# Transposes and value products in pairs, with a score block between, in a fused attention and feed-forward kernel

## The chip, the cores and the metric

The kernel runs on one NeuronCore of a Trainium2 chip. The metric is the device time of one execution in microseconds (us), lower is better. TensorE is PE in the profile, VectorE is DVE, ScalarE is ACT, GpSimd is POOL and SyncE is SP.

## What is computed

One transformer layer on x of 2 batches x 1024 positions x 256 channels, in float32, with adaptive layer norm (the six modulations come from a small input c):

```python
h = _layernorm(x) * (1 + ca) + sa
qkv = einsum('bsh,ph->bsp', h, weight_qkv)         # 4 groups: 4 query heads, 1 key, 1 value, D = 128
scores = einsum('bsgqd,btgd->bgqst', q, k) * D ** -0.5
attn = softmax(where(causal, scores, min))
out = einsum('bgqst,btgd->bsgqd', attn, v)
x = x + ga * (out @ weight_proj.T)
h = _layernorm(x) * (1 + cb) + sb
x = x + gb * ffn(h)                                # two Hadamard transforms, gate and up, silu, down
```

## The kernel before

**Precision.** Every float32 product is made of three matmuls on numbers split in a high and a low part: high x high, high x low, low x high (helper `three`, lines 1127 to 1129, and their like). So everything that TensorE multiplies is first split by two instructions: ACT copies the high part, and DVE subtracts it to get the low one. Transposes are plain float32.

**Turns.** Attention runs in 8 turns (2 batches x 4 key-value groups). One turn holds the queries, keys and values of one group in SBUF. Its 8 rows of 128 positions are taken in four windows, (7,0), (6,1), (5,2), (4,3). A unit (i, j) is row i against key block j for all four heads; there are 36 in a turn, numbered in `UNITS`, 9 in a window. After the turns the feed-forward part runs; the change leaves it alone.

**The walk.** The order of the work is one list, `WALK`, made by `walk()` (line 74). Each engine's program goes through the same list and issues its own share of each item, in order. Items of a turn, written below as in the code with their index:

- C c: chunk c of the next turn's queries, keys (6 matmuls each) or values (12). ACT and DVE split it.
- S i.h: scores of row i, head h (lines 1267 to 1273; 3 or 6 matmuls, row 0 in plain float32 at L1263). DVE takes the maximum (L1040), ACT the exponential (L778), POOL the reciprocal of the sum (L623) and the scaling (L628). There are two score buffers in PSUM, so a score block waits on `exp_done` for the exponential of the block two before it (line 1257; in rows under 4, heads 2 and 3 use the other half and wait for the one four before).
- T n: four transposes of unit n into one of two PSUM banks (L1284). ACT copies it to `pt_hi` (L802), DVE makes `pt_lo` (L1044). The bank is free when `pt_lo` of the unit two before is made; the layer-norm transposes L take a place in the same ring.
- V n: value product of unit n, three matmuls of 512 columns (L1302, L1303, L1305). The first two wait for `pt_hi`, the third for `pt_lo`. After the last unit of a row ACT and DVE split the sum (L819, L1049).
- Y i: output projection of row i, 12 matmuls of 256 columns; DVE adds it to x (L1054). The first of a turn, Y 0, waits on `wp_ready` for the projection weights (line 1311).
- WM and WP: POOL scales the projection weights (L606), and splits them (L614, L616). WP comes before the turn's Y 0.
- VS: ACT and DVE split the values. LF, LN, L, LH, LL: layer norm of two blocks for the feed-forward part: statistics and normalising on DVE, transposes on PE (L), modulation on ACT in the item L (L706), the copy h_hi on DVE in the item LH (L905), the low part on POOL. The bank of L is free when L706 is done. W: POOL splits the next turn's query and key weights (before every second turn the value weights too).

**Exponentials.** ACT doesn't issue the exponential of a score block in that block's item. It keeps it in the list `waiting`, which `exps()` empties: at the next S, C, VS or L item, and after the copy of a T.

**Order before.** A value product follows its transposes at a distance of two units (`LAG = 2`). In the middle of a turn one has S, T n, V n-2, S, T n+1, V n-1, and so on. In the last window the next turn's chunks take the place of the score blocks. In the first turn the items WM and WP stand ahead of the scores of row 7.

Of the kernel before, what the change touches and what calls it, by code (L numbers as in the profile page):

```python
# [70 lines left out]
CHUNKS_AT = [(4, 4, 3, 3), (3, 3, 2, 2)]  # L71


def walk():

# [10 lines left out]
    out += [(0, "C", 9, 0), (0, "WM", 0, 0), (0, "WP", 0, 0), (0, "C", 10, 0)] + s7[:2]  # L91
    out += [(0, "C", 11, 0)] + s7[2:] + [(0, "C", 12, 0), (0, "C", 13, 0)]
    for t in range(TURNS):
        s0, s6 = scores(t, 0), scores(t, NT - 2)
# [3 lines left out]
        behind, due = [], []

        def value():  # L100
            n = behind.pop(0)
            out.append((t, "V", n, 0))
            if due and due[0][0] == 1:
                out.append((t, "Y", due.pop(0)[1], 0))
            for row in due:
                row[0] -= 1
            if n == LAST[UNITS[n][0]]:
                due.append([3 if n >= NU - 3 else 2, UNITS[n][0]])

        for p, pair in enumerate(WINDOWS):  # L110
            units = [n for n, u in enumerate(UNITS) if u[0] in pair]
            fill = [[] for _ in units]
            if p + 1 < NW:
                for k, item in enumerate([item for i in WINDOWS[p + 1] for item in scores(t, i)][p == 0 and t > 0:]):
                    fill[k + (p == 0) * (1 if not t else (k > 1) + (k > 2))].append(item)
            elif t + 1 < TURNS:
                left = [(t + 1, "C", c, 0) for c in range(len(chunks(t + 1)))]
                for k, many in enumerate(CHUNKS_AT[(t + 1) % 2]):
                    fill[k] += left[:many]
                    del left[:many]  # L120
                for h, item in enumerate(scores(t + 1, NT - 1) + scores(t + 1, 0)[:1]):
                    fill[len(CHUNKS_AT[0]) + h].append(item)
                fill[1].append((t + 1, "WM", 0, 0))
            if p == 1:
                for k, what in ((0, "LF"), (3, "LN"), (5, "L"), (6, "LH"), (7, "LL")):
                    fill[k].append((t, what, 0, 0))
# [1291 lines left out]
```

## Time and profile before

| | |
|---|---|
| median of 3 runs | 930.82 us (930.01 to 933.1) |
| the profiled execution's own time | 929.75 us |
| its span, first to last instruction | 927.9 us |
| mean granted TensorE clock | 0.998 of full |
| busy: PE, DVE, ACT, POOL | 98%, 68%, 56%, 53% |
| attention turns | about 47 us to 780 us of the span |

A row of the timeline gives the start in us from the span's start, the time that it took, the engine, the source line, the operation, what it writes and reads, the shape and how many alike are merged. In square brackets stands the idle time of the engine just before it and what ended it. The end of a matmul is modelled and includes its way through the array, so a matmul "takes" 0.27 us and the next one starts 0.11 us after it: the spacing of starts is what a matmul costs TensorE, and a wait shorter than that way through is not listed as idle.

### The profile page before, as it was taken

What the parts mean: (1) busy time and instruction counts of PE and PEld (TensorE: products, weight loads), DVE (VectorE), ACT (ScalarE), POOL (GpSimd) and SP (SyncE); (2) the same over time, 40 slices, a digit from 0 to 9 for tenths busy, and PEclk for the clock granted to TensorE, in tenths of its full rate; (3) what the DMA queues carried; (4) which work ended last, traced back from release to release, by engine and by line L of the source; (5) the groups of instructions that cost most, each with busy time, mean ns of one, the idle gap of its engine ahead of it and who ended that gap; (6) DMA issues with size and microseconds to landing.
All of it is one profiled execution on the core that took longest, in us unless ns stands there. A gap on an engine that the chain in (4) does not pass through costs nothing.

```text
span 927.9 us, 15010 instructions
## 1 busy us (share of the span) xinstructions
PE 911.6 (98%) x5480; PEld 806.3 (87%) x5480; DVE 629.5 (68%) x1297; ACT 515.5 (56%) x1121; POOL 490.0 (53%) x699
## 2 busy tenths in 40 slices
PE   6989999999999999999999999999999999999997
PEld 5888889888898888888888888888888998888886
DVE  6568667865787578647875787378757776764554
ACT  4366556655766576547664766466647667531111
POOL 1576628671867186808671867166727989410000
PEclk9999999999999999999999999999999999999999
DMA  8000100000001000000010000000001001000000
GB/s 283 24 1 2 40 1 24 1 29 1 23 2 40 1 23 1 29 1 23 2 41 1 24 1 29 1 1 24 1 1 69 1 9 67 1 23 0 23 23 23
DMA packets 10180, 21.21 MB, mean 23 GB/s; under 512 B 1280, under 2 KB 5760, under 8 KB 9984
## 3 DMA queue, kind: packets, MB, share of 16 engines
q1 hardware_dynamic: 9392, 20.11, 6.3%
q8 instruction: 41, 0.67, 0.3%
q10 hardware_dynamic: 720, 0.21, 0.1%
q14 instruction: 27, 0.22, 0.1%
HBM read 18.22 MB, written 2.10 MB: 22 GB/s over the span
## 4 chain that ended last, share of the span: by engine, by line
PE 88%; DVE 3%; ACT 2%; POOL 1%; issue 1%; DVEq 0%; POOLq 0%
PE ps L1284 13%; PE ps L1127 12%; PE ps L1129 12%; PE ps L1128 12%; PE ps L1305 6%; PE ps L1302 6%; PE ps L1303 6%; PE ps L1267 6%; PE ps L1273 6%; PE ps L1270 6%; ACT prob L778 1%; DVE ps L1040 1%; ACT pt_hi L802 1%; DVE stats L881 1%; PE ps L1263 1%
## 5 line engine op out<-in xcount | busy, mean ns | idle before, releaser
L623 POOL TENSOR_TENSOR rinv<-rsum,mone 128x1 f32<-128x1 f32 x256 | 141.4, 552 | 232.0 <-ACT prob L778 231.4
L1044 DVE TENSOR_TENSOR pt_lo<-ps,pt_hi 128x512 fp32r<-128x512 f32 x288 | 198.2, 689 | 66.6 <-ACT pt_hi L802 63.4
L802 ACT ACTIVATE pt_hi<-ps 128x512 fp32r<-128x512 f32 x288 | 171.3, 598 | 118.2 <-PE ps L1284 115.8
L778 ACT ACTIVATE prob<-ps,nmax 128x256 f32<-128x256 f32 (+28 forms) x256 | 180.8, 706 | 84.2 <-DVE nmax L1040 82.4
L628 POOL TENSOR_SCALAR prob<-prob,rinv 128x256 f32<-128x256 f32 (+28 forms) x256 | 191.3, 747 | 38.8 <-POOL rinv L623 38.5
L1040 DVE CUSTOM_DVE_ANT_0 ps<-ps,mask_f 128x256 f32<-128x256 f32 (+28 forms) x256 | 183.1, 719 | 37.7 <-PE ps L1273 33.9
L1284 PE MATMUL ps<-ident,prob 128*128 128x128 f32 x1152 | 173.0, 274 | 2.7 <-POOL prob L628 2.4
L1284 PEld LDWEIGHTS ps<-ident,prob 128*128 128x128 f32 x1152 | 140.9, 141 | 22.8 <-DVE pt_lo L1044 4.0
L1302 PE MATMUL ps<-pt_hi,v_hi 128*128 128x512 f32 x288 | 134.3, 466 | 0.0
L1305 PE MATMUL ps<-pt_lo,v_hi 128*128 128x512 f32 x288 | 114.1, 396 | 0.0
L1303 PE MATMUL ps<-pt_hi,v_lo 128*128 128x512 f32 x288 | 113.4, 394 | 0.0
L1267 PE MATMUL ps<-k_hi,q_hi 128*128 128x256 f32 (+16 forms) x352 | 101.1, 346 | 0.6
L1273 PE MATMUL ps<-k_hi,q_lo 128*128 128x256 f32 (+16 forms) x352 | 98.0, 337 | 0.0
L1270 PE MATMUL ps<-k_lo,q_hi 128*128 128x256 f32 (+16 forms) x352 | 97.6, 337 | 0.0
L982 DVE SCALAR_TENSOR_TENSOR q_lo<-ps,q_hi 128x512 fp32r<-128x512 f32 x64 | 44.2, 692 | 53.2 <-ACT q_hi L739 53.1
L1267 PEld LDWEIGHTS ps<-k_hi,q_hi 128*128 128x128 f32 x352 | 63.0, 190 | 15.8 <-ACT prob L778 5.5
L1127 PE MATMUL ps<-wp_hi,o_hi 128*128 128x256 f32 x256 | 73.1, 285 | 0.0
L1129 PE MATMUL ps<-wp_hi,o_lo 128*128 128x256 f32 x256 | 72.4, 283 | 0.0
L1128 PE MATMUL ps<-wp_lo,o_hi 128*128 128x256 f32 x256 | 72.2, 282 | 0.0
L829 ACT ACTIVATE prob<-ps,ws_u 128x512 f32<-128x512 f32 x32 | 22.0, 688 | 87.7 <-PE ps L1129 87.6
L1270 PEld LDWEIGHTS ps<-k_lo,q_hi 128*128 128x128 f32 x352 | 64.1, 189 | 5.3
L1049 DVE TENSOR_TENSOR o_lo<-ps,o_hi 128x512 fp32r<-128x512 f32 x64 | 44.2, 691 | 34.3 <-ACT o_hi L819 34.3
(179 smaller groups left out, 1815.8 us busy)
## 6 DMA issues: line engine op xcount, KB each, us to landing
w_raw<-in_wqkv SPq DMA_DIRECT2D x8, 640.0 KB, 3.9
wp_raw<-in_wproj SPq DMA_DIRECT2D x8, 512.0 KB, 3.5
out_y<-prob SPq DMA_DIRECT2D x8, 256.0 KB, 2.3
x<-in_x SPq DMA_DIRECT2D x3, 512.0 KB, 12.9
prob<-in_wug SPq DMA_DIRECT2D x3, 512.0 KB, 4.0
prob<-in_wmod SPq DMA_DIRECT2D x1, 1024.0 KB, 10.2
wv_raw<-in_wv SPq DMA_DIRECT2D x4, 256.0 KB, 4.3
raw_down<-in_wdn SPq DMA_DIRECT2D x1, 1024.0 KB, 4.8
```

The source lines that it names most:

```text
L628: g_.tensor_scalar(row(i, h), row(i, h), rinv[:, at, h:h + 1], 1.0, ALU.mult, ALU.mult).then_inc(prob_done, 1)
L778: a_.activation(row(i, h).rearrange("p (a n) -> p a n", a=nb), score_banks(i, h).rearrange("p (a n) -> p a n", a=nb)[:, :, 0:w], ACT.Exp, ...
L802: a_.activation(pt_hi[:, n % 3, :], ring(t, "T", n), ACT.Copy).then_inc(pth_done, 1)
L1040: v_.tensor_tensor_reduce(scores, scores, late, -1.0, 3.0e38, ALU.add, ALU.min, nmax[:, place(n), h:h + 1]).then_inc(max_done, 1)
L1044: v_.tensor_tensor(pt_lo[:, n % 3, :], ring(t, "T", n), pt_hi[:, n % 3, :].bitcast(F32), ALU.subtract).then_inc(ptl_done, 1)
L1127: mm(dst, w_h, r_h, start=start, stop=False)
L1128: mm(dst, w_h, r_l, start=False, stop=False)
L1129: return mm(dst, w_l, r_h, start=False, stop=stop)
L1267: mm(dst[:, a * CH:a * CH + wide], queries(q_hi, n, h), k_hi[:, a * w:a * w + wide], start=True, stop=False)
L1270: mm(dst[:, a * CH:a * CH + wide], queries(q_hi, n, h), k_lo[:, a * w:a * w + wide], start=False, stop=False)
L1284: last = tr(ring(t, "T", n)[:, q * P:(q + 1) * P], row(i, q, j * P, (j + 1) * P), ident[:, :])
L1302: mm(O[i], v_hi[:, j, :], pt_hi[:, n % 3, :], start=j == 0, stop=False)
```

## The change

The walk is written anew. Units are taken in pairs g = (2g, 2g+1): what is to stand ahead, T 2g, T 2g+1, what is to stand between, V 2g, V 2g+1, what is to stand behind. The function `put` gives each score block, chunk and layer-norm item a place; an even place n is ahead of pair n/2, an odd one is between the transposes and the value products of pair (n-1)/2. Counted out, turns 1 to 6 read (with | around the pairs' T and V for the eye):

```text
S7.3 V34 V35 Y3 S0.0 S0.1 S0.2 S0.3 VS Y4 WP S6.0 | T0 T1 | S6.1 | V0 V1 | T2 T3 | S6.2 | V2 V3 | T4 T5 | S6.3 Y0 | V4 V5 |
S1.0 | T6 T7 | S1.1 | V6 V7 | S1.2 | T8 T9 | S1.3 S5.0 LF | V8 V9 | S5.1 | T10 T11 | S5.2 Y7 | V10 V11 | LN | T12 T13 | S5.3 | V12 V13 |
S2.0 | T14 T15 | S2.1 LH Y1 | V14 V15 | L S2.2 | T16 T17 | S2.3 LL | V16 V17 | S4.0 | T18 T19 | S4.1 Y6 | V18 V19 | T20 T21 | S4.2 W | V20 V21 |
S4.3 | T22 T23 | S3.0 | V22 V23 | S3.1 | T24 T25 | S3.2 S3.3 Y2 | V24 V25 | T26 T27 | C0 C1 (C2) | V26 V27 | C C WM | T28 T29 | C C Y5 | V28 V29 | ...
```

In the first turn S6 and S1 are each one place later or earlier, and WP stands there: T2 T3 | S6.2 WP | V2 V3 | S6.3 | T4 T5 | S1.0 Y0 | V4 V5. In the last turn the units from 27 on keep the old distance of two. ACT empties `waiting` only after the second T of a pair. Nothing is added to or taken from the set of instructions. The diff, cut to its core (what is left out are the old body of the loop and the last turn's tail):

```diff
@@ -68,16 +68,16 @@
-CHUNKS_AT = [(4, 4, 3, 3), (3, 3, 2, 2)]
+CHUNKS_AT = [(3, 3, 3, 3, 2), (2, 2, 2, 2, 2)]
+
+
+def alone(t, n):
+
+
+    return t == TURNS - 1 and n > LAST[WINDOWS[2][0]] + 1
...
@@ -88,65 +88,64 @@
-    out += [(0, "C", 9, 0), (0, "WM", 0, 0), (0, "WP", 0, 0), (0, "C", 10, 0)] + s7[:2]
+    out += [(0, "C", 9, 0), (0, "WM", 0, 0), (0, "C", 10, 0)] + s7[:2]
     out += [(0, "C", 11, 0)] + s7[2:] + [(0, "C", 12, 0), (0, "C", 13, 0)]
     for t in range(TURNS):
         s0, s6 = scores(t, 0), scores(t, NT - 2)
-        rest = [(t - 1, "Y", i, 0) for i in WINDOWS[-1][::-1]] if t else []
-        out += [(t, "VS", 0, 0)] + s0[3 if t else 0:] + rest[:1] + ([s6[0]] if t else []) + rest[1:]
-        out += [(t, "WP", 0, 0)] if t else []
...
+        if t:
+            out += [(t - 1, "Y", WINDOWS[-1][1], 0)] + s0 + [(t, "VS", 0, 0), (t - 1, "Y", WINDOWS[-1][0], 0), (t, "WP", 0, 0)]
+        else:
+            out += s0 + [(t, "VS", 0, 0)]
+
+        ahead, between, behind = ([[] for _ in range(NU // 2)] for _ in range(3))
+
+        def put(places, items):
+            for n, item in zip(places, items):
+                (between if n % 2 else ahead)[n // 2].append(item)
+
+        put([0, 1, 3, 5] if t else [1, 2, 3, 4], s6)
+        put([6, 7, 8, 9] if t else [5, 6, 7, 8], scores(t, 1))
+        put([9, 10, 11, 13], scores(t, 5))
+        put([14, 15, 16, 17], scores(t, 2))
+        put([18, 19, 21, 22], scores(t, 4))
+        put([23, 24, 25, 25], scores(t, 3))
+        put([9, 12, 15, 17], [(t, what, 0, 0) for what in ("LF", "LN", "LH", "LL")])
+        behind[7].append((t, "L", 0, 0))
+        if t == 0:
+            put([3], [(t, "WP", 0, 0)])
+        if t + 1 < TURNS:
+            put([21], [(t, "W", 0, 0)])
+            left = [(t + 1, "C", c, 0) for c in range(len(chunks(t + 1)))]
+            for k, many in enumerate(CHUNKS_AT[(t + 1) % 2]):
+                put([27 + k] * many, left)
+                del left[:many]
+            put([28], [(t + 1, "WM", 0, 0)])
+            put([32, 33, 34, 35], scores(t + 1, NT - 1))
...
+        due = []
+        for g in range(NU // 2):
+            if alone(t, 2 * g):
+                continue
+            if 2 * g + 1 < NU - 1 and not (t + 1 == TURNS and g == 12):
+                between[g] += [(t, "Y", row, 0) for row in due]
+                due = []
+            due += [UNITS[n][0] for n in (2 * g, 2 * g + 1) if n == LAST[UNITS[n][0]]]
+            out += ahead[g] + [(t, "T", 2 * g, 0), (t, "T", 2 * g + 1, 0)] + between[g]
+            if alone(t, 2 * g + 2):
+                break
+            out += [(t, "V", 2 * g, 0), (t, "V", 2 * g + 1, 0)] + behind[g]
...
@@ -800,7 +799,7 @@
                 if what == "T":
                     act.wait_ge(t_done, this(t_done, t, n + 1))
                     a_.activation(pt_hi[:, n % 3, :], ring(t, "T", n), ACT.Copy).then_inc(pth_done, 1)
-                    if n != NU - 1:
+                    if n % 2 or alone(t, n):
                         exps()
```

## Rows read from the trace of the kernel before

**Rows 1.** The page, part 1: busy time, share and instructions of each engine.

```profile
PE 911.6 (98%) x5480; PEld 806.3 (87%) x5480; DVE 629.5 (68%) x1297; ACT 515.5 (56%) x1121; POOL 490.0 (53%) x699
```

**Rows 2.** Timeline (start us, us, instruction), PE: four transposes standing alone.

```profile
302.63 0.60 PE L1284 MATMUL ps<-ident,prob 128*128 128x128 f32 x4
...
303.30 0.40 PE L1128 MATMUL ps<-h_lo,w_hi 128*128 128x512 f32 x1
```

**Rows 3.** Timeline, PE, eight transposes in a row, where the old order has them.

```profile
147.00 1.04 PE L1284 MATMUL ps<-ident,prob 128*128 128x128 f32 x8
...
148.11 0.39 PE L1303 MATMUL ps<-pt_hi,v_lo 128*128 128x512 f32 x1
```

**Rows 4.** Windows: us, busy us of PE, PEld, DVE, ACT, POOL, then granted clock.

```profile
146.00:149.00 3.00, 3.00 (x20) 2.75 (x20) 2.86 (x6) 2.66 (x5) 2.71 (x4) 1.00 0.00 0
...
45.00:50.20 5.20, 2.82 (x25) 2.61 (x23) 2.16 (x11) 4.08 (x11) 4.79 (x6) 1.00 0.01 4
50.20:54.00 3.80, 3.79 (x13) 3.51 (x14) 1.75 (x3) 1.51 (x6) 3.34 (x10) 0.55 0.00 0
```

**Rows 5.** Timeline, weight loads that waited: the idle time and who ended it.

```profile
154.11 0.42 PEld L1284 LDWEIGHTS ps<-ident,prob 128*128 128x128 f32 x4 [0.24 <-DVE pt_lo L1044]
...
166.29 0.30 PEld L1267 LDWEIGHTS ps<-k_hi,q_hi 128*128 128x128 f32 x2 [0.54 <-ACT prob L778]
```

**Rows 6.** Timeline, PE, two of the twelve matmuls of an output projection.

```profile
299.91 0.28 PE L1128 MATMUL ps<-wp_lo,o_hi 128*128 128x256 f32 x1
300.03 0.28 PE L1129 MATMUL ps<-wp_hi,o_lo 128*128 128x256 f32 x1
```

**Rows 7.** Timeline, ACT and DVE: the copy of a transposed unit and its remainder.

```profile
172.82 0.59 ACT L802 ACTIVATE pt_hi<-ps 128x512 fp32r<-128x512 f32 x1
173.34 0.53 ACT L778 ACTIVATE prob<-ps,nmax 128x320 f32<-128x320 f32 x1
...
303.32 0.59 ACT L802 ACTIVATE pt_hi<-ps 128x512 fp32r<-128x512 f32 x1
...
304.06 0.68 DVE L1044 TENSOR_TENSOR pt_lo<-ps,pt_hi 128x512 fp32r<-128x512 f32 x1
```

**Rows 8.** Groups by line, shapes apart: xcount, busy us, mean ns of one.

```profile
L778 ACT ACTIVATE prob<-ps,nmax 128x256 f32<-128x256 f32 x32 | 15.2, 474 | 10.0 <-DVE nmax L1040 10.0
...
L706 ACT ACTIVATE h<-ps,cols 128x256 f32<-128x256 f32 x28 | 14.2, 558 | 0.0
...
L1054 DVE TENSOR_TENSOR x<-ps,x 128x256 f32<-128x256 f32 x64 | 27.0, 422 | 18.2 <-PE ps L1129 17.4
...
L1040 DVE CUSTOM_DVE_ANT_0 ps<-ps,mask_f 128x352 f32<-128x352 f32 x8 | 4.3, 532 | 0.8
...
L905 DVE CAST h_hi<-h 128x512 fp32r<-128x512 f32 x14 | 6.7, 480 | 1.8 <-ACT h L706 1.8
...
L623 POOL TENSOR_TENSOR rinv<-rsum,mone 128x1 f32<-128x1 f32 x256 | 141.4, 552 | 232.0 <-ACT prob L778 231.4
```

**Rows 9.** Timeline, POOL and ACT: split of wp, scaling of row 7, its exponential.

```profile
38.47 1.05 POOL L614 TENSOR_SCALAR wp_hi<-wp_raw 128x1024 fp32r<-128x1024 f32 x1 [0.19 <-issue]
39.60 2.41 POOL L616 TENSOR_TENSOR wp_lo<-wp_raw,wp_hi 128x1024 fp32r<-128x1024 f32 x1
...
48.14 2.02 POOL L628 TENSOR_SCALAR prob<-prob,rinv 128x1024 f32<-128x1024 f32 x1 [0.21 <-POOL rinv L623]
...
236.33 1.13 POOL L628 TENSOR_SCALAR prob<-prob,rinv 128x1024 f32<-128x1024 f32 x1 [0.21 <-POOL rinv L623]
...
45.08 1.12 ACT L778 ACTIVATE prob<-ps,nmax 128x1024 f32<-128x1024 f32 x1 [0.25 <-DVE nmax L1040]
```

**Rows 10.** Timeline, PE, first turn: the awaited transpose and a later score block.

```profile
50.21 0.33 PE L1284 MATMUL ps<-ident,prob 128*128 128x128 f32 x1 [2.39 <-POOL prob L628]
...
56.00 0.56 PE L1267 MATMUL ps<-k_hi,q_hi 128*128 128x432 f32 x2
...
57.18 0.60 PE L1284 MATMUL ps<-ident,prob 128*128 128x128 f32 x4
```

More of the change, by code:

```diff
@@ L94, in walk @@
         s0, s6 = scores(t, 0), scores(t, NT - 2)
-        rest = [(t - 1, "Y", i, 0) for i in WINDOWS[-1][::-1]] if t else []
-        out += [(t, "VS", 0, 0)] + s0[3 if t else 0:] + rest[:1] + ([s6[0]] if t else []) + rest[1:]
-        out += [(t, "WP", 0, 0)] if t else []
[L98 to L126, printed above, removed]
-            if p == 2 and t + 1 < TURNS:
-                fill[3].append((t, "W", 0, 0))
-            if p == 3 and t == 1:
-                for k in range(5):
-                    fill[k + 3].append((t, "GB", k, 0))
-            if t + 1 == TURNS and p < 3:
-                fill[(6, 4, 4)[p]].append((t, "B", p, 0))
-            if t + 1 == TURNS and p == 3:
-                fill[5].append((t, "H", 0, 0))
-            for n, extra in zip(units, fill):
-                transposes = [item for item in extra if item[1] == "L"]
-                extra = [item for item in extra if item[1] != "L"]
-                out += extra[:1] + [(t, "T", n, 0)] + extra[1:]
-                behind.append(n)
-                if len(behind) > LAG:
-                    value()
-                out += transposes
@@ L144, in walk @@
-        while behind:
-            if len(behind) == LAG and t + 1 < TURNS:
-                value()
-                out += scores(t + 1, 0)[1:3]
-            value()
-        assert [i for _, i in due] == list(WINDOWS[-1][::-1])
+        if t:
[3 more added lines that the diff above has]
+        ahead, between, behind = ([[] for _ in range(NU // 2)] for _ in range(3))
@@ new lines, in walk @@
+        behind[7].append((t, "L", 0, 0))
[9 more added lines that the diff above has]
+            put([32, 33, 34, 35], scores(t + 1, NT - 1))
+            if t == 1:
+                put(range(30, 35), [(t, "GB", k, 0) for k in range(5)])
+        else:
+            put([6, 13, 22], [(t, "B", k, 0) for k in range(3)])
@@ L150, in walk @@
+        if t + 1 == TURNS:
+            first = LAST[WINDOWS[2][0]] + 2
+            for n in range(first, NU):
+                out += [(t, "T", n, 0)] + ([(t, "H", 0, 0)] if n == 32 else []) + [(t, "V", n - 2, 0)]
+                if n - 2 == LAST[WINDOWS[2][0]]:
+                    due = [(t, "Y", WINDOWS[2][0], 0)]
+                elif n == first + 2:
+                    out += due
+            out += [(t, "V", NU - 2, 0), (t, "V", NU - 1, 0)]
     for n, i in enumerate(WINDOWS[-1][::-1]):
```

## Prediction

> **What bounds the kernel now.** I read the page first. PE is busy 98% of the span, no other engine over 68% [rows 1]. That figure includes each matmul's way through the array, so I went on to the timeline of PE and read the spacing of starts. A matmul of 256 columns costs 0.12 us [rows 6], one of 512 columns 0.23 us (worked out below); between them I take the column's share. Over the attention turns nearly every start follows the last at its spacing. What is left is small waits, too short to be listed as idle on PE, that show where a weight load stood still: the transposes T 6 behind a `pt_lo` (0.24 us idle), the scores S 5.3 behind an exponential (0.54 us, of which PE lost 0.27) [rows 5]. Adding such gaps over one middle turn I get some 1.2 us. The one large wait is in the first turn: the last transpose of T 0 waits 2.39 us for POOL, which had split `wp` before it scaled row 7 [rows 9, 10], and the clock then falls (0.55 over 3.80 us, after 1.00) [rows 4]. So PE's stream is the path, and each wait added to it adds its whole length. All waits there are make about 8 x 1.2 + 2.5 + 1.7 = 14 us, which is all that a new order can win unless the work itself gets cheaper.
>
> **Does pairing make the work cheaper?** Four transposes alone and the matmul behind them take 303.30 - 302.63 = 0.67 us from first start to the start after [rows 2]. Eight in a row with the same matmul behind them take 148.11 - 147.00 = 1.11 us [rows 3]. The difference, 0.44 us, is what four more transposes cost: 0.109 us each, and in the first figure 0.67 - 4 x 0.109 = 0.23 us is left for the matmul, its ordinary spacing. So passing from matmuls to transposes and back costs nothing that pairing could save: 144 passages fewer, at 0.00 us (at most 0.01 by the rounding of the rows, 1.4 us in all). The same holds for V next to V, where no row shows a spacing other than 0.23 us.
>
> The Trainium skill (TensorE: Matmul & The Clock Gate, Part 4) says that transposes don't count as PE being busy for the clock gate. A pair puts 0.87 us of them in a row; in the stretch with the eight the granted clock was 1.00 [rows 4], so the trace speaks against a cost here. By that rule the clock could fall; that is a rival below.
>
> **The new distance.** Before, V n came two units after T n. Now it comes behind one block. From the start of T n: `pt_hi` starts 0.69 us later and takes 0.59; the next instruction on ACT can start 0.52 after it (173.34 - 172.82); `pt_lo` starts 0.03 to 0.15 after `pt_hi` is done and takes 0.68 [rows 7]. So for a pair starting at 0, `pt_hi` is there at 1.28 and 1.80, `pt_lo` at about 2.05 and 2.7. PE reaches the third matmul of V 2g at 0.87 + block + 0.46, that of V 2g+1 0.69 later. With a block of 0.7 us or more (rows 6, 5, 7, the chunks, anything with a Y of 12 x 0.12 = 1.44 us) nothing waits. With a short one:
> - V 6 behind S 1.1 (3 x 0.12 = 0.36 us): 2.05 - 1.69 = **0.4 us**.
> - V 22 behind S 3.0 (about 0.58): **0.2 us**.
>
> **Exponentials put off.** ACT empties its list only behind the second `pt_hi` of a pair, so an exponential of the block ahead starts at about 1.7. Who waits for it:
> - S 5.0 needs that of S 1.2, which stands right ahead of T 8. 1.7 + 0.47 [rows 8] + 0.1 for reading the sum = 2.3; PE is there at 0.87 + 0.36 = 1.23. **1.05 us**, in turns 1 to 7. In the first turn S 1.3 stands elsewhere and this wait isn't there.
> - C 1 needs that of S 3.3: 1.7 + 0.8 = 2.5 against 0.87 + six matmuls (1.38): **0.25 us**, in 7 turns.
> - At the turn's end ACT takes the split of row 4 behind V 35, a copy of the shape of `pt_hi`, and then the exponential of S 7.3 (1.12 [rows 9]). S 0.1 needs it. Counted from V 35's end: copy started at 0.2, exponential from 0.75 to 2.0; PE comes there after Y 3 and S 0.0 at 1.55. **0.4 us.**
>
> **LH ahead of L.** In the new order LH is queued on DVE ahead of Y 1's add and the items of the next pair, yet it waits for L706, whose transposes L come behind V 14 and V 15. From L's start: L706 begins at 0.69, takes 2 x 0.56 less an overlap of 0.1 [rows 8], so T 17, which has the bank of L, may start at 1.75. PE is there after L, S 2.2 and T 16, 0.44 + 0.50 + 0.44 = 1.38: **0.35 us.** DVE then has the copy (0.44), the add (0.42), the maximum (0.53) [rows 8] and `pt_lo` (0.68) before V 16's third matmul: ready at 1.75 + 2.05 = 3.8. PE comes at 1.75 + 0.44 + 0.54 + 0.46 = 3.2: **0.6 us.**
>
> **Sum of a middle turn.** New waits 0.4 + 0.2 + 1.05 + 0.25 + 0.4 + 0.35 + 0.6 = 3.25 us; old waits that go (T 6, S 5.3, T 15, those about S 6.1, S 6.2 and S 0.3) 1.2 us. Net +2.05; six such turns +12.3. The last turn has no C 1: 3.0 - 1.1 = +1.9. The first has neither S 5.0's nor the end of a turn before it: 1.8 - 0.55 = +1.25. The other moves are free: W now stands ahead of S 4.3's scaling, but T 27 comes 12 us later; WP of turns 1 to 7 is done before Y 0 by over 2 us.
>
> **The first turn's WP.** POOL is freed of 1.05 + 2.41 us [rows 9] ahead of row 7. What then decides is the exponential of S 7.3, done at 45.08 + 1.12 + 0.1 for reading the sum = 46.3; reciprocal [rows 8], gap and scaling (0.55 + 0.21 + 1.13) bring the last part of row 7 to 48.3 to 48.6 (its 2.02 us in the old trace fell beside the value split, which now comes later; 1.13 is the ordinary figure [rows 9]). T 0 finishes 1.5 us earlier. The clock: 3.80 us at 0.55 lost 1.7 us [rows 4]; with a wait of 1.1 us instead of 2.5 I take it that it stays up: -1.6. V 0 then finds `pt_lo` late behind the value split, +0.4.
> The price is at Y 0. WP is queued behind the scaling of S 6.2. Its exponential stands on ACT behind V 3's copy: V 3 ends 1.4 us after S 6.2, then 0.2 + 0.55 for the copy and 1.1 for the exponential; scaling 0.08 + 0.55 + 0.21 + 0.97 (864 columns, where 1024 take 1.13); WP 0.1 + 1.05 + 2.41 with 0.1 between. `wp_ready` comes at 1.4 + 1.85 + 1.8 + 3.6 = 8.65 us after S 6.2's end. PE reaches Y 0 after V 2 and V 3 (1.4), S 6.3 (1.2, as 57.18 - 56.00 [rows 10]), T 4 and T 5 (0.87), S 1.0 (0.36): 3.85. **A wait of 4.8 us**, longer than the one after which the clock fell, so another 1.6 us lost to the clock. Behind Y 0 on PE stands all the rest of the walk, V 4 first. Net of the first turn's start: -1.5 - 1.6 + 0.4 + 4.8 + 1.6 = +3.7.
>
> **Total:** 12.3 + 1.9 + 1.25 + 3.7 = +19 us on the profiled execution's 929.75: 949. That execution is 1.1 under the median, so the forecast for the median is **950 us**.
>
> **Bounds.** Middle turns: if ACT, DVE and semaphores are each as quick as their best rows, 2.6 us of new waits and 1.4 of old ones go (+1.2 a turn); if each wait pushes the next, 4.5 against 1.0 (+3.5). Start: from +1 (no second fall of the clock, WP early by a slot of ACT) to +6 (first fall stays too). Together +10 to +33, 940 to 963.
>
> **Rivals.**
> 1. *The new waits are mostly absorbed* (an engine that PE waits for runs on meanwhile, and the next wait is gone; I counted them one by one). Then the turns come out within 0.5 us of before and only Y 0 is left: 930.8 + 4 + 3 = 938, between 933 and 942. For it: ACT and DVE are free a third of the time. Against: S 5.0's and T 17's waits come from the order of the lists and not from load.
> 2. *Faster.* Y 0's wait is the one mechanism: it decides when `wp_ready` comes within 1 us of Y 0's turn, which needs the scaling of S 6.2 some 4 us earlier than I have it. Then the start gains 3.1 - 1 = 2 us, and with turns that lose nothing, or lose their old 1.2, the time is 921 to 928. Against: 3.5 us of POOL work doesn't fit in 3.85 us behind an exponential that isn't started yet.
> 3. *The clock falls with long runs of transposes.* One stretch of 1.7 us a turn on top: 950 + 8 x 1.7 = 964. Against it the clock row above; the rule of the page named there is what speaks for it.
> 4. *Nothing changes:* PE's stream is the same and the waits only move. Within 3 us of 931.
>
> **Chances.** Forecast (942 to 958) 0.64; rival 1 0.13; rival 2 0.09; over 958, rival 3 with it, 0.08; rival 4 0.06. A measurement of this kernel can tell about 0.3% (2.8 us) from no change. So faster 0.09, same 0.06, slower 0.85. The range 934 to 959 leaves out about 2 in 10.
>
> **What would show it.** In the profile after: spacing of L1284 still 0.109 us in runs of eight; a weight load L1127 of Y 0 idle for some 4 to 5 us in the first turn with POOL L616 as its releaser, and a second place with a low clock; S 5.0's load (L1267, 336 columns) waiting on an exponential of 256 columns once a turn; the copy L905 on DVE idle before it for some 2 us a turn and a late third matmul L1305 behind it; T 0 ready near 48.6 us. The prediction is wrong if PE's work itself shrinks (a spacing of transposes under 0.10 us), or if the turns keep their old length.

## The result, and the profile after

The changed kernel takes 959.16 us (median of 6 runs, 958.24 to 960.16), the kernel before 930.80 us (6 runs). The ratio is 1.0304 with a 95% interval of 1.0291 to 1.0317: 28.4 us slower, where +19 was forecast. The direction was right. The time lies 0.16 us above 959, the upper end of the stated range (934 to 959), and above the 942 to 958 that got 0.64; it lies inside the bounds of 940 to 963. The profiled execution took 959.26 us with a span of 957.4 us, against a span of 927.9 us before. The numbers of lines up to 1304 are one lower than in the kernel before.

The page's part 1 of the changed kernel (busy us, share, instructions), to be read against [rows 1]:

```profile
PE 920.9 (96%) x5480; PEld 808.3 (84%) x5480; DVE 617.0 (64%) x1297; ACT 508.3 (53%) x1121; POOL 487.0 (51%) x699
```

Not one instruction more, and DVE, ACT and POOL are each a little less busy than before. What was added is waiting. These are the waits of PE in the changed kernel (engine, line, releaser: us in total, times, longest), without two at the start that both kernels have. Of those shown the kernel before has only the transposes' wait on POOL, once, 2.4 us.

```profile
PE ps L1266 <- ACT prob L777: 8.3, 15, 0.8
...
PE ps L1126 <- POOL wp_lo L615: 4.5, 1, 4.5
PE ps L1304 <- DVE pt_lo L1043: 2.5, 9, 0.8
PE ps L1283 <- POOL prob L627: 2.2, 2, 1.4
PE ps L1283 <- ACT h L705: 2.0, 8, 0.3
...
PE ps L1262 <- ACT prob L777: 1.5, 7, 0.3
PE ps L1126 <- DVE pt_lo L1067: 1.2, 2, 0.6
PE ps L1233 <- DVE v_lo L1002: 0.6, 1, 0.6
PE ps L1283 <- DVE pt_lo L1043: 0.3, 1, 0.3
```

They come to 23.1 us, and they leave out what is hidden in a matmul's way through the array. So I sized each wait as the prediction did: a start less the start that the ordinary spacing would have given. For S 5.0 in turn 2:

```profile
267.94 0.28 PE L1272 MATMUL ps<-k_hi,q_lo 128*128 128x256 f32 x1
269.06 0.57 PE L1266 MATMUL ps<-k_hi,q_hi 128*128 128x336 f32 x2 [0.84 <-ACT prob L777]
```

The start at 269.06 should have been 267.94 + 0.12 = 268.06, so 1.00 us is lost, and 0.09 more in the spacings behind it. That second part was not expected: behind nearly every wait, the next matmul of another weight starts about 0.1 us late. At S 2.1:

```profile
181.03 0.41 PE L1266 MATMUL ps<-k_hi,q_hi 128*128 128x320 f32 x1 [0.31 <-ACT prob L777]
...
181.14 0.19 PEld L1269 LDWEIGHTS ps<-k_lo,q_hi 128*128 128x128 f32 x1
181.28 0.31 PE L1269 MATMUL ps<-k_lo,q_hi 128*128 128x320 f32 x1
...
181.43 0.31 PE L1272 MATMUL ps<-k_hi,q_lo 128*128 128x320 f32 x1
```

L1269 comes 0.25 us behind L1266, where L1272 comes 0.15 behind L1269: its weight load began at 181.14 only, after the wait, so no earlier matmul ran beside it.

Summed in this way over all matmuls, turn 0 grew by 4.9 us, turn 1 by 3.6, turns 2 to 6 by 2.42 to 2.54 each (12.3), turn 7 by 5.5, the feed-forward part by 2.4, and the start up to S 0.0 by 0.7. That is 29.4 of the 29.5 us between the spans; where a turn is taken to end moves up to 0.4 us of it from one turn to the next. The work itself cost the same in both. With each width of matmul at its median spacing, taken in each kernel by itself, all matmuls together come to 896.4 us before and 895.9 after: pairing neither saves nor costs TensorE anything that can be seen.

### The profile page after: what moved, and what is told of

It is laid out like the page before. It is cut to its first block, busy times and chain, and to the rows that moved or that the text cites. A ratio compares the mean times of both kernels' runs of the same rounds, so it can differ in the third digit from the quotient of the medians.

```text
span 957.4 us, 15010 instructions
## 1 busy us (share of the span) xinstructions
PE 920.9 (96%) x5480; PEld 808.3 (84%) x5480; DVE 617.0 (64%) x1297; ACT 508.3 (53%) x1121; POOL 487.0 (51%) x699
## 4 chain that ended last, share of the span: by engine, by line
PE 84%; ACT 6%; DVE 5%; POOL 3%; issue 1%; DMA 0%; SPq 0%; DVEq 0%; POOLq 0%; ACTq 0%
PE ps L1126 12%; PE ps L1127 11%; PE ps L1128 11%; PE ps L1283 10%; PE ps L1304 7%; PE ps L1301 6%; PE ps L1302 6%; PE ps L1266 6%; PE ps L1272 5%; PE ps L1269 5%; ACT prob L777 2%; ACT pt_hi L801 1%; ACT o_hi L818 1%; ACT h L705 1%; DVE pt_lo L1043 1%
## 5 line engine op out<-in xcount | busy, mean ns | idle before, releaser
L1043 DVE TENSOR_TENSOR pt_lo<-ps,pt_hi 128x512 fp32r<-128x512 f32 x288 | 185.7, 684 | 64.3 <-ACT pt_hi L801 64.0
L801 ACT ACTIVATE pt_hi<-ps 128x512 fp32r<-128x512 f32 x288 | 158.2, 598 | 124.2 <-PE ps L1283 122.6
L1283 PE MATMUL ps<-ident,prob 128*128 128x128 f32 x1152 | 152.8, 273 | 4.8 <-POOL prob L627 2.2
L1283 PEld LDWEIGHTS ps<-ident,prob 128*128 128x128 f32 x1152 | 133.6, 140 | 19.0 <-ACT h L705 3.9
L1266 PE MATMUL ps<-k_hi,q_hi 128*128 128x256 f32 (+16 forms) x352 | 108.8, 368 | 8.3 <-ACT prob L777 8.3
L1301 PE MATMUL ps<-pt_hi,v_hi 128*128 128x512 f32 x288 | 115.5, 401 | 0.0
L1272 PE MATMUL ps<-k_hi,q_lo 128*128 128x256 f32 (+16 forms) x352 | 97.6, 336 | 0.0
L1269 PE MATMUL ps<-k_lo,q_hi 128*128 128x256 f32 (+16 forms) x352 | 97.3, 335 | 0.0
L1304 PEld LDWEIGHTS ps<-pt_lo,v_hi 128*128 128x128 f32 x288 | 54.3, 188 | 26.5 <-DVE pt_lo L1043 13.4
L1266 PEld LDWEIGHTS ps<-k_hi,q_hi 128*128 128x128 f32 x352 | 59.8, 190 | 16.2 <-ACT prob L777 11.6
L1269 PEld LDWEIGHTS ps<-k_lo,q_hi 128*128 128x128 f32 x352 | 63.8, 188 | 4.1
```

Source lines behind the costliest of these rows:

```text
L1043: v_.tensor_tensor(pt_lo[:, n % 3, :], ring(t, "T", n), pt_hi[:, n % 3, :].bitcast(F32), ALU.subtract).then_inc(ptl_done, 1)
L1266: mm(dst[:, a * CH:a * CH + wide], queries(q_hi, n, h), k_hi[:, a * w:a * w + wide], start=True, stop=False)
L1269: mm(dst[:, a * CH:a * CH + wide], queries(q_hi, n, h), k_lo[:, a * w:a * w + wide], start=False, stop=False)
L1283: last = tr(ring(t, "T", n)[:, q * P:(q + 1) * P], row(i, q, j * P, (j + 1) * P), ident[:, :])
L1301: mm(O[i], v_hi[:, j, :], pt_hi[:, n % 3, :], start=j == 0, stop=False)
L1304: mm(O[i], v_hi[:, j, :], pt_lo[:, n % 3, :], start=False, stop=j == i).then_inc(pv_done, 1)
```

## Point by point, from the trace

| step of the forecast | forecast, us | trace after, us |
|---|---|---|
| S 5.0, turns 1 to 7 | 1.05 | 1.09 |
| V 6 (and V 7 behind it) | 0.4 | 0.31 + 0.10 |
| V 22 (and V 23) | 0.2 | 0.10 + 0.10 |
| T 17 | 0.35 | 0.47 |
| V 16 (and V 17) | 0.6 | 0.34 + 0.11 |
| C 1 | 0.25 | 0.22 to 0.30 |
| S 0.1 | 0.4 | 0.36 to 0.42 |
| S 2.1, every turn | none | 0.57 |
| T 27 in turns 1, 3, 5; Y 4 | none | 0.21; 0.08 |
| old waits of a middle turn that go | 1.2 | 1.4 |
| V 34, V 35 in turn 1 | none | 0.97 + 0.11 |
| T 30 and T 35 in the last turn | none | 1.91 + 0.49 |
| T 0 | 1.1 | 1.01 |
| V 0 (and V 1) in the first turn | 0.4 | 0.17 + 0.11 |
| Y 0 in the first turn, POOL's part | 4.8 | 4.7 |
| clock after Y 0 | 1.6 | about 2.1 |
| feed-forward start | none | 2.4 |

The waits that were worked out are all there, with the releaser named and within 0.15 us, but for the clock. Here is the chain of POOL that ends in Y 0, which [rows 9] and [rows 10] had to be put together for:

```profile
59.92 0.99 POOL L627 TENSOR_SCALAR prob<-prob,rinv 128x864 f32<-128x864 f32 x1 [0.21 <-POOL rinv L622]
60.88 1.05 POOL L613 TENSOR_SCALAR wp_hi<-wp_raw 128x1024 fp32r<-128x1024 f32 x1
62.01 2.34 POOL L615 TENSOR_TENSOR wp_lo<-wp_raw,wp_hi 128x1024 fp32r<-128x1024 f32 x1
...
64.40 0.58 PE L1126 MATMUL ps<-wp_hi,o_hi 128*128 128x256 f32 x1 [4.47 <-POOL wp_lo L615]
```

Windows of the changed kernel (us, busy PE, granted clock, DMA share, GB/s):

```profile
56.00:60.00 4.00, 3.93 (x24) 1.00 0.00 0
60.00:64.00 4.00, 0.00 (x0) 0.78 0.01 2
64.00:68.00 4.00, 3.60 (x15) 0.50 0.40 131
68.00:72.00 4.00, 4.00 (x22) 0.87 0.00 0
72.00:76.00 4.00, 4.00 (x26) 1.00 0.00 0
```

TensorE stands still from 60 to 64.4 us. The granted clock falls to 0.50 (1.2 GHz) at about 62.3, still within the wait, and is back at 1.00 at about 69.1: 6.8 us, of which TensorE works in 4.7. In the kernel before [rows 4] it was low from about 50.6 to 54.0, 3.4 us, all of it behind the wait. That the low stretch is twice as long doesn't follow from the longer wait alone: in the profiles of lh_late, s5_apart, exp_13 and b2_late (below), with the same wait of 4.46 to 4.47 us, the clock fell just behind the wait's end and was low for 3.4 us, and Y 0's own matmuls lost 0.3 to 0.5 us less. In the changed kernel Y 0 lost 1.1 us in its own twelve matmuls, V 4 and V 5 another 1.0.

What was missed has three kinds.

**One consumer of the late exponentials was left out.** I asked who waits for an exponential that is held back behind the second `pt_hi`. At S 2.1 another copy stands ahead of it, that of o_hi behind V 13. ACT in turn 1:

```profile
179.50 0.60 ACT L818 ACTIVATE o_hi<-ps 128x512 fp32r<-128x512 f32 x1 [0.95 <-PE ps L1304]
179.99 0.90 ACT L777 ACTIVATE prob<-ps,nmax 128x768 f32<-128x768 f32 x1
```

ACT is idle for 0.95 us with the exponential of S 5.3 in its list, because the next item in its program is that copy. Eight times 0.57 is 4.6 us.

**The last turn wasn't walked.** There the item B 2 (the feed-forward weights' butterfly, sums and differences of their halves) now stands ahead of the scaling of all four heads of row 3. In the kernel before, the scaling of S 3.0 was done first, and B 2 began 9.1 us ahead of T 30; now it begins 7.8 us ahead of it. POOL:

```profile
785.53 1.29 POOL L584 TENSOR_TENSOR dif_down<-w_raw 128x512 f32<-128x512 f32 x1
786.79 1.30 POOL L585 TENSOR_TENSOR w_raw<-w_raw 128x512 f32<-128x512 f32 x1
788.18 0.62 POOL L591 TENSOR_SCALAR w_hi<-dif_down 128x512 fp32r<-128x512 f32 x1
788.77 0.62 POOL L591 TENSOR_SCALAR w_hi<-w_raw 128x512 fp32r<-128x512 f32 x1
...
795.52 0.33 PE L1283 MATMUL ps<-ident,prob 128*128 128x128 f32 x1 [1.39 <-POOL prob L627]
```

These 3.9 us come out as 1.9 us at T 30 (b2_late below tests it). In turn 1 it is DVE that is behind, with the modulations (GB), at V 34.

**A part that the change doesn't touch grew.** In the feed-forward start TensorE stops three times, 2.4 us in all, for one subtraction on DVE. It makes a low part of the gated values, which lies in the buffer `pt_lo`, from two operands in SBUF. The same subtraction took 0.68 us in the kernel before. DVE and POOL of the changed kernel:

```profile
816.39 4.62 DVE L1067 TENSOR_TENSOR pt_lo<-prob,pt_hi 128x512 fp32r<-128x512 f32 x1
...
815.42 1.30 POOL L584 TENSOR_TENSOR dif_down<-prob 128x512 f32<-128x512 f32 x1
816.67 1.29 POOL L585 TENSOR_TENSOR prob<-prob 128x512 f32<-128x512 f32 x1
817.92 1.29 POOL L598 TENSOR_TENSOR w_lo<-dif_down,w_hi 128x512 fp32r<-128x512 f32 x1
819.17 1.29 POOL L598 TENSOR_TENSOR w_lo<-prob,w_hi 128x512 fp32r<-128x512 f32 x1
```

DVE's operation ends 0.55 us after the last of the four. Before, the two engines came together at 789.34 and 789.35, and there it was POOL's that took longer:

```profile
789.34 0.68 DVE L1068 TENSOR_TENSOR pt_lo<-prob,pt_hi 128x512 fp32r<-128x512 f32 x1
...
789.35 1.82 POOL L586 TENSOR_TENSOR prob<-prob 128x512 f32<-128x512 f32 x1
```

Counted from the first Hadamard matmul (780.04 before, 807.09 after) DVE's operation starts at 9.30 us in both kernels, and POOL's at 9.31 before and at 9.58 after. So the two programs met 0.27 us apart from where they met before, and that went with which of the two waited. The Trainium skill (SBUF — State Buffer, section "SBUF: two separate sides") says that a DVE operation with two SBUF inputs and a GpSimd operation share one pair of ports, that who starts first has it for the whole instruction and that the other blocks. The rows of both kernels agree with the blocking. But here DVE stood through four instructions of POOL and not one. At the next such subtraction of the kernel before it stood through one only (DVE at 792.97, 1.27 us long), and then it was POOL's next, at 793.72, that took 1.67 us.

## The experiments

Fifteen kernels were run beside the kernel before. Each ratio is to the runs of the kernel before in the same batch, whose medians were 930.22 to 931.16 us. The first group takes the causes one by one, on the changed kernel.

**wp_early** puts the split of the projection weights back where it was (the diffs here are cut to their core):

```diff
-(0, "WM", 0, 0), (0, "C", 10, 0)
+(0, "WM", 0, 0), (0, "WP", 0, 0), (0, "C", 10, 0)
-            put([3], [(t, "WP", 0, 0)])
```

> The changed kernel with the first turn's WP put back ahead of the scores of row 7; all else as changed. Changed kernel: 959.2 us. Theory (the time is the sum of the waits in PE's stream): the waits of the changed kernel that belong to the late WP go, namely Y 0's 4.6 us, about 2.3 us of low clock behind it, the 1.0 us at T 0 and 0.3 us at V 0, and the old one at T 0 comes back with its low clock (2.55 + 1.9 us). Net -3.8 us: 955.4, between 954 and 957. Rival (the wait at Y 0 is absorbed by later waits, so that taking it away only uncovers others): 958 to 960. Rival (the clock is what costs, and falls again behind T 0 for just as long): 956 to 958.

952.84 us, ratio 1.0223 to 1.0257: 6.3 less. That is more than the theory's 954 to 957 allowed. Y 0's wait is gone, as it said, but T 0 waits 1.51 us and not 2.39, and the low clock that it had come back doesn't. The clock stays at 1.00:

```profile
50.22 0.77 PE L1281 MATMUL ps<-ident,prob 128*128 128x128 f32 x5 [1.51 <-POOL prob L625]
```

**lh_late** gives LH place 16 (with T 16, T 17) in place of 15. **s5_apart** gives S 5 the places 10 to 13 from turn 1 on, so that S 5.0 isn't right behind S 1.3:

```diff
-        put([9, 12, 15, 17], [(t, what, 0, 0) ...
+        put([9, 12, 16, 17], [(t, what, 0, 0) ...
```
```diff
-        put([9, 10, 11, 13], scores(t, 5))
+        put([10, 11, 12, 13] if t else [9, 10, 11, 13], scores(t, 5))
```

> The changed kernel with the item LH (DVE's copy h_hi) moved behind the item L and S 2.2. Theory: DVE no longer stands idle for 2.9 us ahead of it, the add of Y 1 and the maximum of S 2.2 are done in that time, and V 16's third matmul stops waiting (0.46 us a turn); T 17's wait for the bank of L (0.47 us a turn) stays, since ACT's L706 sets it. 8 x -0.46 = -3.7 us: 955.5, between 954.5 and 957. Rival (both waits come from LH's place): 8 x -0.93 = -7.4 us: 951 to 953. Rival (V 16 then waits for pt_hi behind L706 all the same): 958 to 960.

> The changed kernel with S 5.0 put behind V 8 and V 9 in turns 1 to 7, instead of right behind T 8, T 9 and S 1.3. Theory (a wait costs its length and 0.1 us for the load behind it that nothing hid): S 5.0's wait of 1.09 us a turn goes; but V 8 then stands behind a block of 0.36 us only, as V 6 does, and waits 0.31 + 0.1 us. 7 x (-1.09 + 0.41) = -4.8 us: 954.4, between 953.5 and 956. Rival (no new wait at V 8): -7.6, 951 to 952.5. Rival (the wait moves to S 5.1, whose buffer is just as late): 957 to 960.

954.67 us (ratio 1.0245 to 1.0279) and 955.57 us (1.0257 to 1.029), both in the range of their theories. With LH later, V 16's and V 17's waits are gone and T 17's stays at 0.47. With S 5 apart, its wait is gone and V 8 and V 9 wait 0.31 + 0.10. (The single runs of s5_apart lie between 954.3 and 957.06, so its gain is less certain than the other. In both, some 0.5 us of the gain is the shorter stretch of low clock behind Y 0, which the edits don't touch.)

**exps_each** lets ACT empty its list after each transposed unit, as before; **exps_first** empties it ahead of every o_hi copy; **exp_13** ahead of V 13's alone:

```diff
-                    if n % 2 or alone(t, n):
+                    if n != NU - 1:
                         exps()
```
```diff
                     i = UNITS[n][0]
+                    exps()                       # exp_13: if n == 13
                     act.wait_ge(pv_done, ...)
```

> The changed kernel with ACT emptying its list of exponentials behind every T again, not only behind the second of a pair. Theory (waits come from the order of the lists on ACT and DVE): S 5.0's exponential starts 0.5 us earlier, so its wait falls from 1.1 to 0.6 us, and C 1's from 0.3 to 0; but the second pt_hi of each pair then stands behind an exponential of 0.5 to 1.1 us, so the third matmul of V 7, V 23 and V 33 waits 0.4, 0.9 and 0.4 us more. Net +1.0 us a turn: 962 to 967. Rival (putting the exponentials off is itself what costs, as in the prediction's list): the waits at S 5.0, C 1 and S 0.1 shrink by 1.2 us a turn and nothing else moves: 949 to 952.

> The changed kernel with ACT emptying its list also right ahead of the copy o_hi behind the last V of a row. That takes away the cause of two waits: S 2.1 for the exponential of S 5.3, which stands behind the copy for V 13 (0.57 us a turn), and S 0.1 for that of S 7.3 (0.36 to 0.42 us). Theory (each wait goes alone): -7 us, 951 to 953. Rival (the copy then comes late itself, and the output projection right behind, Y 1 and Y 4, waits 0.5 to 0.7 us for o_lo instead): no difference, 958 to 961.

> The changed kernel with the exponentials put off taken up before the o_hi copy behind V13 alone (in the run before they were taken up before every such copy). Theory (S2.1's wait of 0.57 us and the 0.1 us behind it hang on this one place in ScalarE's queue): S2.1's wait falls under 0.1 us in all eight turns, 4 to 5.5 us less: 954 to 955.5. Rival (the copy, now 0.4 us later, holds up the Y or the next pt_hi and the wait is given back): 957 to 961.

All three theories fell: 989.72 us (ratio 1.062 to 1.0656), 976.12 (1.0475 to 1.051) and 961.32 (1.031 to 1.0354). The rivals' ranges were passed as well (exp_13's by 0.3 us). In exps_first and exp_13 S 2.1's wait does fall, from 0.57 to 0.07 us (in exps_each it stays, and S 5.0's falls to 0.6), but what was put behind the exponential now waits instead. In exp_13 Y 1 is late by 0.76 us in all eight turns. This line of its waits shows it (the o_hi of V 13 makes Y 1's operand). Behind it stands, for comparison, a line of exps_each, whose value products wait for `pt_hi`:

```profile
PE ps L1128 <- DVE o_lo L1050: 4.0, 8, 0.5
```
```profile
PE ps L1301 <- ACT pt_hi L801: 3.1, 7, 0.5
```

With pairs, two of ACT's copies are due within 0.87 us of each other and the value product follows at once. An exponential of 0.5 to 1.1 us has no place between them that nobody waits for. So the list emptied only behind the second copy, which looks like the cause of the waits at S 5.0, C 1, S 0.1 and S 2.1, is the cheapest of the four rules tried here.

**b2_late** gives B 2 the place 26 in place of 22.

> The changed kernel with the last turn's item B 2 (3.8 us of POOL, preparing the first feed-forward weights) moved from ahead of the scaling of row 3 to behind it. Theory: T 30's last transpose waits 1.9 us in the last turn because POOL does B 2 first; that wait and the 0.5 us at T 35 go, and POOL's later work starts no later than now, since the sum ahead of it is the same: 959.2 - 1.9 to - 2.4, 956.5 to 957.5. Rival (the feed-forward part waits for what B 2 prepares, and the gain is given back there): 958.5 to 960.

959.97 us (1.0303 to 1.0335). The theory's 956.5 to 957.5 was missed; the time is the rival's, but the gain is given back at another place than it named. T 30's wait is gone and so is the feed-forward start's 2.4 us. But ACT's copy of a feed-forward weight's high part (`raw_high`, ahead of the `pt_hi` of T 33 in its list) then waits 3.36 us for POOL's butterfly, and T 35 on TensorE waits with it:

```profile
803.00 1.11 PE L1283 MATMUL ps<-ident,prob 128*128 128x128 f32 x4 [3.32 <-DVE pt_lo L1043]
```
```profile
800.00:804.00 4.00, 1.00 (x5) 0.72 0.00 0
804.00:808.00 4.00, 4.00 (x12) 0.50 0.55 202
```

The clock falls once more. All that was won is given back.

**pairs_far** puts the value products one pair later (four `pt` buffers in place of three; to make room `scb` shares `raw_down` and `ws_row` shares `dif_dn`):

```diff
+            out += [(t, "V", n, 0) for n in (2 * g - 2, 2 * g - 1) if g]
             if alone(t, 2 * g + 2):
                 break
-            out += [(t, "V", 2 * g, 0), (t, "V", 2 * g + 1, 0)] + behind[g]
+            out += behind[g]
```

> The changed kernel with the value products of a pair a whole pair later (T 2g, T 2g+1, block, V 2g-2, V 2g-1), which takes a fourth buffer for pt_hi and pt_lo (one F32 helper and one row of weights share space with others for it, with no instruction more). It keeps the pairing and takes the short distance away. Theory (pairing costs and saves nothing on PE; distance causes the waits at V 6, V 7, V 16, V 17, V 22, V 23 and in turn 1 at V 34): of these 8 x 1.2 + 1 = 10.6 us some 9 go, and those from the order of lists (S 5.0, S 2.1, T 17, C 1, Y 0, T 30) stay: 949 to 952. Rival (pairs gain on PE once the waits are gone): below 945. Rival (pairs themselves are what costs): 957 to 960.

961.26 us (1.0314 to 1.0346): the theory (949 to 952) fell, and the time of the rival that blames the pairs themselves (957 to 960) was passed. No V waits any more and S 2.1, S 0.1 neither, and Y 0 waits 0.9 us only with the clock at 1.00 throughout; yet as much came back: T 2 and T 3 lose 1.2 us in most turns, S 1.1 0.7, and T 17 1.0 in place of 0.47. Waits of PE in it:

```profile
PE ps L1274 <- ACT prob L785: 9.0, 14, 0.8
PE ps L1291 <- POOL prob L635: 6.0, 12, 0.8
PE ps L1291 <- ACT h L713: 6.0, 8, 0.7
...
PE ps L1291 <- DVE pt_lo L1051: 1.9, 8, 0.3
```

L1291 are the transposes. Two in a row need two free banks and two scaled blocks at one moment, and there are two banks and two score buffers. The distance of the value products was thus not the only tight one: with pairs the transposes' own inputs are. The kernel before wasn't given the fourth buffer, so what the buffer alone does is not known.

**four_undone** joins WP, LH, S 5 and three units' advance of GB. **train_cut** tests the 4.62 us: one wait more on POOL, between the two operations of the last butterfly.

```diff
                 g_.tensor_tensor(raw_sum[sum_slot(n)], a, b, ALU.add)
+                if n == PIECES[5]:
+                    pool.wait_ge(g_ok, 1)
                 g_.tensor_tensor(b, a, b, ALU.subtract)...
```

**six_undone** joins these five and exp_13's edit.

> The changed kernel with four of its places set back or shifted, the pairs of transposes and of value products kept: WP before C10 as in the kernel before, LH one place later, the score block S5 one place on, the GB items three units earlier. Theory (each wait has its own cause and they add): 952.8 us of the kernel with WP alone set back, less 4.5 for LH, 3.6 for S5 and 1 for GB: 943.5 us, 942.5 to 945.5. What is left then, 13 us over the kernel before, is S2.1, T17, V6, C1, S0.1 and the waits behind row 3's scaling, which hang on the pairs themselves. Rival (the waits come back elsewhere, as they did where B2 was moved): 948 to 953 us.

> The changed kernel with one wait more, on GpSimd in the feed-forward start: the second operation of the last piece's butterfly waits until VectorE has made the first pt_lo of the gate (L1067). In the changed kernel that pt_lo takes 4.62 us and ends with the end of four GpSimd operations that ran without a gap; TensorE waits for it three times, 2.4 us in all. Theory (the GpSimd operations hold VectorE's two-operand subtraction off as long as one follows the other): the subtraction takes about 1 us, TensorE's three waits are gone, 2.2 to 2.6 us less: 956.8 us, 956 to 957.5. Rival (the 4.62 us come from something else, such as the instruction transfer at 824 us, or GpSimd's wait makes the fifth piece's operands late): 959 to 961.

> The changed kernel with all the places found: WP, LH, S5, GB as before, the cut in GpSimd's row of operations, and the exponential ahead of V13's copy. Theory (the causes add): 944.3 us of the kernel with the first four, less 2.4 and less 4.5 to 5: 937.3 us, 936.5 to 938.5. What is left over the kernel before is then some 7 us: T17, V6 and V7, S0.1, C1 and the last turn. Rival (they share ScalarE's queue): 940 to 943.

four_undone: 944.32 us (1.0137 to 1.0168), 0.8 above the point forecast and inside its range: these causes add. train_cut: 957.50 us (1.0267 to 1.0305), 1.7 less than the changed kernel. Its runs, 957.13 to 958.74, lie around the end of the theory's range, and its interval overlaps the changed kernel's, so the time alone doesn't settle it. The trace does: POOL is idle and DVE is through in 0.91 us, though POOL's operation before still runs for the first 0.36 of them:

```profile
817.98 0.91 DVE L1069 TENSOR_TENSOR pt_lo<-prob,pt_hi 128x512 fp32r<-128x512 f32 x1
...
817.00 1.34 POOL L584 TENSOR_TENSOR dif_down<-prob 128x512 f32<-128x512 f32 x1
818.97 1.30 POOL L587 TENSOR_TENSOR prob<-prob 128x512 f32<-128x512 f32 x1 [0.63 <-DVE pt_lo L1069]
```

From the first Hadamard matmul to the last matmul of the kernel it takes 143.05 us, the changed kernel 145.16, the one before 142.71: 2.1 of the 2.4 us are back. The rest is a later `pt_lo`, 1.72 us, that met POOL again. The profiled execution as a whole won less than that, since TensorE's wait for the first weights took 7.0 us there and 6.2 in the changed kernel's. six_undone: 947.48 us (1.0156 to 1.0202), above the theory (936.5 to 938.5) and the rival (940 to 943), a miss by exp_13's edit: Y 1 waits 0.76 us eight times and S 2.1 still 0.35 in seven turns.

The second group takes the first turn's order alone, on the kernel before.

**old_wp_late** moves WP ahead of T 0 and nothing else. **old_start** also puts VS behind S 0, as the change does. **old_ln_late** gives LF, LN, L, LH, LL the units 3, 5, 6, 7, 8; **old_both** is the last two together.

```diff
-        out += [(t, "VS", 0, 0)] + s0[3 if t else 0:] + ...
+        out += ([(t, "VS", 0, 0)] + s0[3:] if t else s0 + [(t, "VS", 0, 0), (t, "WP", 0, 0)]) + ...
```

> The kernel before with one edit: the first turn's WP stands behind the scaling of row 0 (ahead of T 0) instead of ahead of the scores of row 7. Its Y 0 stands seven units later, behind V 5. Theory: T 0's wait falls from 2.55 to 1.0 to 1.8 us (the value split on DVE still stretches the scaling of S 7.3), the clock stays up as it did in the run with WP put back (-1.6 to -1.9), and Y 0 doesn't wait, since WP is done at about 57.5 us and Y 0 comes at 63. 930.3 - 2.7 = 927.6, between 926.5 and 928.5. Rival (POOL is late for rows 6 and 1 then, and T 9 waits): 929.5 to 932.

> The kernel before with the change's order of the first turn's start alone: all of S0, then the value split VS, then the projection weights' split WP, and no transposes or value products put together. Theory (the order of the start, not the place of WP alone, decides what the first exponentials wait for): T0's wait falls from 2.39 us to about 1.0, the wait of S6.0's first weight load, 2.4 us with WP alone moved, is gone because its exponential is no longer behind the value split on ScalarE, and the granted clock stays up through 50 to 60 us: 2.5 to 3.5 us less, 926.5 to 928 us. Rival (the wait only moves on to the next block, or Y0 now waits for POOL's split as in the changed kernel): within 0.1% of before, 929.5 to 931.5 us. Were Y0 to wait 4.7 us with the clock down after it, it is slower, 933 to 937.

> The kernel before with the four LayerNorm items of a turn one to three units later: LF, LN, L, LH, LL at units 3, 5, 6, 7, 8 in place of 0, 3, 5, 6, 7; nothing else differs. Theory (each wait of the stream is one item's due time, and can be taken away by that item's place): the wait of S5.3 (0.37 us in a turn) is gone, 7 times that is 2.6 us less, 927.5 to 928.5 us. Rival (the later items take ScalarE's and VectorE's time where the transposes and score blocks stand, so that the wait reappears there): 930 to 933 us.

> The two edits above together in the kernel before. Theory (the waits are separate and add): the sum of the two, 924 to 926 us. Rival (they share ScalarE's queue and do not add, or each only moves its wait): 928 to 932 us.

| kernel | median, us | ratio to before, 95% |
|---|---|---|
| old_wp_late | 931.36 | 0.9999 to 1.0017 |
| old_start | 927.33 | 0.9955 to 0.9979 |
| old_ln_late | 931.17 | 1.0000 to 1.0018 |
| old_both | 928.89 | 0.9976 to 0.9994 |

Only old_start came out as its theory said; old_wp_late, old_ln_late and old_both took the times of their rivals. In old_wp_late T 0's wait falls from 2.39 to 0.84, and a new one of 2.01 comes behind it. In old_start that one is 0.23 us:

```profile
50.20 0.33 PE L1284 MATMUL ps<-ident,prob 128*128 128x128 f32 x1 [0.84 <-POOL prob L628]
52.54 0.64 PE L1267 MATMUL ps<-k_hi,q_hi 128*128 128x400 f32 x2 [2.01 <-ACT prob L778]
```
```profile
50.02 0.33 PE L1284 MATMUL ps<-ident,prob 128*128 128x128 f32 x1 [0.84 <-POOL prob L628]
54.38 0.66 PE L1267 MATMUL ps<-k_hi,q_hi 128*128 128x432 f32 x2 [0.23 <-ACT prob L778]
```

The exponential that S 6.0 waits for stood behind the value split on ACT. With both moved, the clock is 1.00 in every window from 46 to 66 us, and the kernel is faster than the one before by 0.33%. That is the one part of the change that was seen to pay, and it was so on the old order, where Y 0 comes behind V 5 and WP isn't up against it. old_ln_late shows the rule of the middle turns on the old order: S 5.3's wait is gone, and T 17 waits 0.40 us in every turn for the bank of L in its place, so nothing is won.

## Why the prediction was right and wrong

**What held.** That PE's stream is the path and that pairing makes its work no cheaper: the spacing in runs of eight stayed, and so did the sum of ordinary spacings. That each new wait adds its whole length: wp_early, lh_late and s5_apart gave back 6.3, 4.5 and 3.6 us by the medians (6.0, 3.9 and 2.9 by the ratios within each batch). For LH the sum had 8 x 0.6 = 4.8; for S 5.0 it had 7 x 1.05 less what V 8 takes back. That Y 0 waits for POOL. The first turn came out at 4.9 us against 1.25 + 3.7, but that is partly luck: S 2.1's 0.57 and 0.5 us of low clock behind Y 0 were missing in it, and smaller waits at V 0 and V 16 and 0.3 us more of old low clock that went made up for most of them.

**Which step failed.** The sum of the waits, which was not complete; most terms in it were right. "New waits ... = 3.25 us" left out S 2.1 (0.57), T 27 (0.2 in every second turn) and Y 4 (0.08). T 27 was among "The other moves are free": in turn 1 W holds POOL from 200.07 to 206.36 us, S 4.3's scaling ends at 207.87 behind it, and the last transpose of T 27 starts at 207.93, 0.2 us late. Behind the waits that it had, the 0.1 us of the unhidden load was missing, which the smaller size of some of them made up for. A middle turn came to +2.5 for +2.05, and turn 1 to +3.6: 3.6 us over the six. "The last turn has no C 1" took the last turn as a middle one less a wait. Its walk also puts B 2 ahead of all of row 3's scaling in POOL's queue, and it came to +5.5 for +1.9. And the feed-forward part was taken as unchanged, +2.4 for 0. These three are 9.6 of the 10.3 us by which the spans' difference passed the sum, and the last 0.7 is the time up to S 0.0, which differed between the two executions ahead of anything that the change moves. The bounds of the middle turns (+1.2 to +3.5) held; no bound was set on the last turn and on the part behind it.

**The rivals.** Rival 1, that the waits are absorbed, didn't happen. Rival 2 didn't: Y 0's wait was 4.7 us. Rival 4, that nothing changes, didn't. Rival 3 gave 964, nearer to 959.16 than the forecast of 950, for a reason that isn't there. The clock was 1.00 in the stretches with runs of eight, and the spacing there 0.109 us, so the rule of the Trainium skill (TensorE: Matmul & The Clock Gate, Part 4) that was weighed there costs nothing in this kernel (timeline of PE, then a window with its granted clock):

```profile
150.17 1.03 PE L1283 MATMUL ps<-ident,prob 128*128 128x128 f32 x8
...
165.66 1.03 PE L1283 MATMUL ps<-ident,prob 128*128 128x128 f32 x8
...
165.00:167.00 2.00, 2.00 (x17) 1.00 0.00 0
```

**What stays open.** With the four causes undone the kernel is still 1.4 to 1.7% over the one before. By the spacing, S 2.1 (4.5 us), T 17 (3.8), V 6 and V 7 (3.3), V 8 and V 9 (2.9), S 0.1 (2.5), the last turn (2.4), the feed-forward start (2.4), C 1 (1.8) and V 22 and V 23 (1.6) come to some 25 us; against them stand some 12 us of old waits and low clock that are gone, which leaves about the 14 us that were measured. pairs_far and the three kernels with other places for the exponentials speak for it that most of these hang on the pairs; no kernel here removed them all, so that is argued and not shown. The times of the feed-forward start don't belong to the pairs as such: in b2_late, with all pairs kept, they were gone. Why POOL held DVE off through four operations stays open. train_cut shows that a gap ends it. But that a row of POOL's operations has no gap isn't the whole cause: in train_cut DVE's next subtraction, at 821.61, stood through one of them and got in ahead of the next, which was then POOL's to wait (1.76 us in place of 1.30).

## What to carry over

Where one engine's stream is the path and is gapless, regrouping its own instructions wins nothing if their spacing doesn't shrink, and it takes slack from all that feeds them: two operands are due at once where there was time between. Walk the last round and the part behind it item by item, queue by queue, like the middle one; here they held 6 of the 10 us that were missed. And a wait taken away by another order in one engine's program can come back at the next consumer, as in exps_first, exp_13, b2_late and old_ln_late, so judge an edit by the sum of the waits, not by the one that it removes.

## What the runs showed of the hardware

- Behind a wait of TensorE the next matmul with new weights starts about 0.1 us late (0.25 us in place of 0.15 at S 2.1); its weight load, too, began only after the wait (181.14, the awaited matmul at 181.03).
- The granted clock stayed at 1.00 after single waits of 0.84, 1.39 and 1.51 us, and fell with waits of 2.39, 3.32 and 4.47 us, and after 0.84 and 2.01 us close together. How long it was low didn't follow the wait's length: 3.4 us with the 2.39 us, and with the same 4.46 to 4.47 us either 6.8 us (the changed kernel, about 62.3 to 69.1; exps_each, train_cut) or 3.4 us (lh_late, s5_apart, exp_13, b2_late).
- A subtraction of two SBUF operands on VectorE took 4.62 us in place of 0.68 beside four gapless GpSimd operations. Where the two started together, it was GpSimd's that took 1.82 us in place of 1.30. At other places of the same programs VectorE's stood through one GpSimd operation only (1.27 us in the kernel before, 1.72 in train_cut).
